# A two-layer attention kernel: a reordered opening, and VectorE adds the row of maxima to five groups of sixteen in 27 inner blocks of layer 0

## The reference, cut to what matters

```
# layer 0
theta = theta_w @ x + theta_b      # 64 x 4096, queries
phi   = phi_w @ x + phi_b          # 64 x 4096, keys
g     = g_w @ x + g_b              # 64 x 4096, values
y     = softmax(theta^T phi) @ g^T
x     = W_w @ y^T + W_b + x
# layer 1
q, k, v = Wq @ x + bq, Wk @ x + bk, Wv @ x + bv
x     = x + (softmax(q^T k * 128**-0.5) @ v^T)^T
```

## Time and profile before

| | us |
|---|---|
| median of 3 runs | 3208.1 (3196.96 to 3208.27) |
| the profiled execution, its time | 3209.59 |
| the profiled execution, its span | 3207.8 |
| busy PE / POOL / DVE / ACT in the span | 3171.6 / 2916.0 / 2104.9 / 1828.9 |

### The profile page before, as it was taken

How to read it: one execution, slowest core, us unless ns; L and a number is a source line. 1 busy time by engine, 2 the same in 40 slices (tenths; PEclk the granted TensorE clock), 3 DMA queues, 4 the chain that set the end, 5 groups by cost and what they waited for, 6 DMA issues and landing times. The chain is left out here.

```text
span 3207.8 us, 42372 instructions
## 1 busy us (share of the span) xinstructions
PE 3171.6 (99%) x15748; PEld 2088.9 (65%) x15748; DVE 2104.9 (66%) x2588; ACT 1828.9 (57%) x2378; POOL 2916.0 (91%) x1546
## 2 busy tenths in 40 slices
PE   8999999999999999999999999999999999999997
PEld 4555555547777765555777776555577777777775
DVE  4555555557777765555777776555577777777773
ACT  3545455555666655554666665555466666666665
POOL 3999999988999999998899998999899999999997
PEclk9999999999999999999999999999999999999999
DMA  1000000005756640000665654000066675657575
GB/s 52 21 27 27 24 27 27 27 27 109 144 115 140 136 99 21 27 27 27 128 141 112 144 119 102 27 27 24 26 142 129 132 145 114 134 118 145 114 141 119
DMA packets 91934, 271.68 MB, mean 85 GB/s; under 512 B 10192, under 2 KB 10192, under 8 KB 91728
## 3 DMA queue, kind: packets, MB, share of 16 engines
q0 software_dynamic: 55296, 201.35, 32.5%
q1 hardware_dynamic: 36432, 67.62, 7.1%
HBM read 50.83 MB, written 16.78 MB: 21 GB/s over the span
## 5 line engine op out<-in xcount | busy, mean ns | idle before, releaser
L1134 POOL TENSOR_TENSOR p_lo<-probs,p_hi 128x1024 fp32r<-128x1024 f32 x448 | 1160.9, 2631 | 110.3 <-ACT probs L895 76.3
L390 POOL TENSOR_TENSOR sums<-sums,probs 128x1024 f32<-128x1024 f32 x448 | 1067.5, 2383 | 104.5 <-ACT probs L901 53.3
L991 DVE TENSOR_REDUCE piece_max<-rough 128x2 f32<-128x1024 f32 x504 | 616.8, 1224 | 463.1 <-PE rough L546 463.0
L901 ACT ACTIVATE probs<-scores 128x1024 f32<-128x1024 f32 x512 | 519.7, 1025 | 638.3 <-PE scores L579 619.2
L1015 DVE TENSOR_TENSOR probs<-scores,shift_rows 128x1024 f32<-128x1024 f32 x512 | 626.6, 1224 | 369.7 <-PE scores L592 362.0
L894 ACT ACTIVATE p_hi<-probs 128x1024 fp32r<-128x1024 f32 x448 | 475.0, 1060 | 569.2 <-DVE probs L1015 568.9
L985 DVE TENSOR_REDUCE piece_max<-rough 128x1 f32<-128x512 f32 x1024 | 661.9, 683 | 125.8 <-PE rough L540 125.8
L895 ACT ACTIVATE probs<-probs 128x1024 f32<-128x1024 f32 x512 | 535.3, 1046 | 89.1 <-DVE probs L1015 89.1
L588 PE MATMUL scores<-qry_a,keys_a 128*128 128x512 f32 x1024 | 441.9, 432 | 0.0
L1168 POOL DMA_DIRECT2D sent_sums<-probs x384 | 409.2, 1066 | 0.0
L592 PE MATMUL scores<-qry_b,keys_a 128*128 128x512 f32 x1024 | 400.1, 391 | 0.0
(11 more groups left out here) (97 smaller groups left out, 4041.0 us busy)
## 6 DMA issues: line engine op xcount, KB each, us to landing
sent_sums<-probs POOLq DMA_DIRECT2D x384, 512.0 KB, 4.9
x_q<-x SPq DMA_DIRECT2D x32, 256.0 KB, 2.8
x_res<-x SPq DMA_DIRECT2D x32, 256.0 KB, 3.2
mid<-mid_new SPq DMA_DIRECT2D x32, 256.0 KB, 2.4
x_kv<-mid SPq DMA_DIRECT2D x32, 256.0 KB, 2.9
x_q<-mid SPq DMA_DIRECT2D x32, 256.0 KB, 2.8
x_res<-mid SPq DMA_DIRECT2D x32, 256.0 KB, 4.7
out<-result SPq DMA_DIRECT2D x32, 256.0 KB, 3.8
```

The costliest lines, as they stand in the source:

```text
L390: eng.tensor_tensor(sums[:], sums[:], probs[:, slot(st, s)], ALU.add).then_inc(s_plus, 1)
L901: nc.scalar.activation(probs[:, slot(st, s)], scores[:, s % 2], ACT.Exp, scale=SCALES[0]).then_inc(s_whole, 1)
L991: nc.vector.reduce_max(piece_max[:, t, TPG * c:TPG * (c + 1)], src, AX.X).then_inc(s_reduced, 1)
L1134: nc.gpsimd.tensor_tensor(dst, w, rd(hi), ALU.subtract).then_inc(done, 1)
```

## The change

A table `MOVED = (2, 6, 8, 12, 14)` names five groups. In the blocks of layer 0 whose next block is also of layer 0 and whose previous block is not of layer 1 (8 + 7 + 6 + 6 = 27 of the 32 blocks of layer 0) these groups get three products instead of four. DVE adds `shift_rows` on the way from PSUM to `probs` (`move_scores`), and ACT takes exp in place there (`probs_moved`). PE may write the PSUM buffer again when DVE has read it (`s_moved`). A pair inside a group (s = 5 and 11) now stands behind the third product instead of the second, in all blocks with such pairs.

The opening is written anew: the constants come in two DMAs (330 columns first, 640 later), the first queries are projected from x part 0, PE runs two products on constant tiles first and three more later that nothing reads (`busy`), pairs stand between the projections from the first chunks on, and the two small products move behind the next queries.

```diff
+MOVED = (2, 6, 8, 12, 14)
+        self.moved = MOVED if self.layer == 0 and self.by_pair and self.prev != 1 else ()
...
+                elif st.layer == 0 and s - 2 in st.moved:
+                    pe.wait_ge(s_moved, moved_until(st.g, s - 2))
...
-                    for n, (keys, qry) in enumerate(((hi[:, k], qa), (lo[:, k], qa), (hi[:, k], qb),
-                                                     (share[:], shift_rows[:, parity]))):
+                    products = [(hi[:, k], qa), (lo[:, k], qa), (hi[:, k], qb)]
+                    if s not in st.moved:
+                        products.append((share[:], shift_rows[:, parity]))
...
-                        if n == 2 and between is not None:
+                        if n == 3 and between is not None:
...
+            def probs_moved(st, s):
+                act.wait_ge(s_moved, moved_until(st.g, s))
+                place = probs[:, slot(st, s)]
+                nc.scalar.activation(place, place, ACT.Exp, scale=SCALES[0]).then_inc(s_whole, 1)
...
+            def move_scores(st, s):
+                dve.wait_ge(s_scores, st.g * GROUPS + s + 1)
+                probs_free_0(dve, st, s)
+                dve.wait_ge(s_row_sb, st.g + 1)
+                nc.vector.tensor_tensor(
+                    probs[:, slot(st, s)].rearrange("p (h c) -> p h c", c=QB),
+                    scores[:, s % 2].rearrange("p (h c) -> p h c", c=QB),
+                    rd(shift_rows[:, st.parity]).unsqueeze(1).to_broadcast([P, TPG, QB]), ALU.add).then_inc(s_moved, 1)
...
+            pe.wait_ge(s_set, 1)
+            pe.wait_ge(s_fill, 1)
+            busy(2)
+            pe.wait_ge(s_const, 16)
+            pe.wait_ge(s_x0[0], 16)
+            project(rough[:, 0:QB], wt_theta, first_image(0), p_q)
+            first_phi(0)
+            first_phi(1)
+            for c in range(0, BLOCKS, 2):
+                first_pair(2 * c)
+                first_g(c)
+                first_pair(2 * c + 1)
+                first_g(c + 1)
+                first_pair(2 * c + 2)
+                if c + 2 < BLOCKS:
+                    first_phi(c + 2)
+                    first_pair(2 * c + 3)
+                    first_phi(c + 3)
+                else:
+                    pe.wait_ge(h_phi, BLOCKS)
+                    busy(1)
+                    first_pair(2 * c + 3)
+                    busy(2)
+            pe.wait_ge(s_ones_r, 1)
             shift_row(0, 0)
             pe.wait_ge(s_reduced, PAIRS + 1)
             next_queries(1, 0, rough[:, 0:QB])
+            small_products()
```

More of the change, by code:

```diff
@@ L358, in probs_free_1, with moved_until @@
                 eng.wait_ge(s_plus, added(st.prev_nth, last))
+        def moved_until(g, s):
+            n = 0
+            for at in range(g + 1):
+                t, i = divmod(at, BLOCKS)
+                turn = (t >= 3 and i == 0) or (t >= 1 and i == BLOCKS - 1)
+                if layer_of(t) == 0 and not turn:
+                    n += len(MOVED) if at < g else MOVED.index(s) + 1
+            return n
         def shifted(nth, s):
@@ L427, in _ @@
         def _(sp):
-            sp.dma_start(const_sb[:], consts).then_inc(s_const, 16)
+            early = sum(w for _, w in CONST_PARTS[:FIRST_CONSTS])
+            sp.dma_start(const_sb[:, 0:early], consts[:, 0:early]).then_inc(s_const, 16)
             for k in range(X_PARTS):
                 sp.dma_start(probs[:, k], cols(x[0], k, GC)).then_inc(s_x0[k], 16)
-                if k == 0:
-                    sp.dma_start(x_q[:], cols(image(x, 0), 0)).then_inc(s_xq, 16)
+                if k == 1:
+                    sp.dma_start(const_sb[:, early:], consts[:, early:]).then_inc(s_late_const, 16)
             def load_q(g, layer, b, i):
@@ L579, in score_group @@
                             last = mm(scores[:, s % 2, h * QB:(h + 1) * QB], keys[half(h)], qry[half(h)],
-                                      start=n == 0, stop=n == 3)
+                                      start=n == 0, stop=n == len(products) - 1)
                     last.then_inc(s_scores, 1)
@@ L667, in out_projection, with small_products, busy, first_phi @@
                 mm(acc_out[:, parity], wt_out, o_sb[:], start=True, stop=True).then_inc(s_wy, 1)
[L670 to L688, removed]
+            def small_products():
+                pe.wait_ge(s_late_const, 16)
+                mm(rough[:, QB:QB + 2], wk, ones[:, 0:2], start=True, stop=True)
+                mm(rough[:, QB + 2:QB + 4], wt_out, g_bias, start=True, stop=True).then_inc(s_small, 1)
+            def busy(n):
+                for _ in range(n):
+                    mm(scores[:, 0, 0:QB], ones[:], total[:], start=True, stop=True)
+            def first_phi(c):
                 if c >= 2:
                     pe.wait_ge(h_phi, c - 1)
-                    pe.wait_ge(h_g, c - 1)
                 if c % 2 == 0:
@@ L907, in _ @@
             act.wait_ge(s_const, 16)
-            act.wait_ge(s_vec, 2)
             take_q_hi(0, 0, 0, rough[:, 0:QB])
-            for c in range(BLOCKS):
-                if c >= 2:
-                    act.wait_ge(l_phi, c)
-                take_phi(c, 0, c, scores[:, c % 2, 0:QB], (whole, x_kv)[c % 2])
-                take_g(c, g_first, c, scores[:, c % 2, QB:GC])
+            for c in range(0, BLOCKS, 2):
+                for n in (c, c + 1):
+                    if n >= 2:
+                        act.wait_ge(l_phi, n)
+                    take_phi(n, 0, n, scores[:, n % 2, 0:QB], (whole, x_kv)[n % 2])
+                for n in (c, c + 1):
+                    take_g(n, g_first, n, scores[:, n % 2, QB:GC])
             shift_to_row(0, 0)
             take_q_hi(1, 0, 1, rough[:, 0:QB])
+            act.wait_ge(s_vec, 2)
             def block_program(st):
@@ L945, in block_program @@
                         take_output(g, parity)
-                    if st.layer == 0:
+                    if s in st.moved:
+                        probs_moved(st, s)
+                    elif st.layer == 0:
                         probs_direct(st, s)
@@ L1078, in _ @@
                 reduce_pair(m, pair, pair_banks[m % 2])
+                if m == 0:
+                    dve.wait_ge(s_late_const, 16)
+                    nc.vector.tensor_scalar(neg_ident[:], idt, -1.0, None, ALU.mult).then_inc(s_neg, 1)
+            dve.wait_ge(s_neg, 1)
             shift(0, 0)
+            dve.wait_ge(s_small, 1)
+            nc.vector.tensor_copy(K_S, rough[:, QB:QB + 1]).then_inc(s_vec, 1)
+            nc.vector.tensor_tensor(OUT_B, rough[:, QB + 2:QB + 3], vec[:, 7:8], ALU.add).then_inc(s_vec, 1)
+            dve.wait_ge(s_vec, 2)
             split_q(1, 0, 1, rough[:, 0:QB])
@@ L1107, in block_program @@
                         m += 1
+                    if s in st.moved:
+                        move_scores(st, s)
                     if st.layer == 1:
```

39 lines of the change are left out of this document (25 added, 14 removed).

## The result

The changed kernel took 3285.47 us as a median of 4 runs (3277.27 to 3285.75), against 3208.18 (3196.96 to 3209.16) before: a ratio of 1.0243, 95% interval 1.0222 to 1.0263. It is 77 us slower. The executions of the kernel before fall into two groups, and in the 48 that were timed beside the experiments 32 lie at 3208.0 to 3210.7 and 16 at 3196.2 to 3198.1; the profiled one is of the longer kind. The direction and the two gaps were forecast; the size, 3257 with a range of 3212 to 3282, was not.

A forecast was written before the change was run, and what follows sets the result against it. PE was taken to bound the kernel, busy 99% of the span. From 3208.1 us, new gaps less saved products add 60.5 over 27 blocks and the opening gains 12: 3256.6 us, range 3212 to 3282.

The forecast's parts named there:

- the two gaps: New PE waits in a layer 0 block: 1.6 us at the next block's first pair, 1.5 us at group 9.
- The bound and its reading: Layer 0 inner blocks: PE busy 41.0 of 41.0 us, so any chain through DVE and ACT that lengthens opens a gap.
- The saving: Five products fewer on PE at 0.23 us each: 1.16 us a block, 31 us over 27 blocks.
- Group 14 and the block's end: Add behind `diag` delays both exps, the row and the queries; next block's first pair waits 1.6 us.
- the knock-on of 12: Groups 12 and 13: 0.25 us gap at group 15, plus 0.1 to 0.2 on the block-end chain; together 0.4 us.
- Groups 6 and 7: Add of 6 behind the reciprocals, exp of 7 behind four diagonals: group 9 waits, gap 1.5 us a block.
- The sum of a later block: New gaps of 3.5 us minus 1.16 saved: each block 2.3 us longer, between 1.2 and 2.7.
- The opening: the step that failed: Products on constants lift PE to the upper clock level: first score at 38 instead of 49.98, a 12 us gain.
- The forecast's low case: Opening stays at the lower clock level: a gain of only 4 us, total 3265.
- POOL: POOL's own block of about 40.2 us stays hidden, waiting more than 2 us a block after the change.
- The rival of a single gap: Only one of the two large block gaps opens: 3218 or 3205 us, counted as no change; chance 0.10.
- the rival of the middle: Only the gap at groups 6 and 7 opens: 0.3 us a block, 3205 us; within a shared chance of 0.10.

The follow-up runs named there:

- three groups: Kernel before, with its old opening, with only groups 2, 8 and 12 moved: 3198.5 us, ratio 0.9972.
- g first: Changed kernel, but in stage 0 ACT copies the g projection ahead of exp of group 14: 3268.4 us, ratio 1.0199.
- the add first: Changed kernel, but DVE adds group 6 ahead of the reciprocals and ACT writes the diagonals one group later: 3272.2 us, ratio 1.0212.
- without constants: Changed kernel with groups 2, 8, 12 moved (stage 0: 2 and 8) and no products on constants in the opening: 3200.9 us, ratio 0.9984.
- the three groups with the new opening: Changed kernel with groups 2, 8 and 12 moved in later blocks, only 2 and 8 in stage 0: 3194.7 us, ratio 0.9957.

## Why the prediction was wrong

*The bound and its reading.* Right. PE without a gap and chains with under 1 us of slack: each of these turned into a gap once it got 1.2 us longer.

*The saving.* Right: 0.23 us a product. The block with no group moved was 0.1 shorter besides (40.86 instead of 40.95); its one change is the place of the pair, which I had set to nothing.

*Group 14 and the block's end, later stages.* Right in place and size. Without group 14 the later block loses 1.6 us (43.50 to 41.90), the product of 0.23 given back included; 1.6 plus the knock-on of 12, less that product, had been worked out.

*Groups 6 and 7.* Right: 1.4 us a block (43.50 to 42.11) for 1.5 - 0.23.

*The sum of a later block.* 2.3 forecast, 2.55 measured (43.50 - 40.95). By the three runs with a group left out, group 14 cost 1.8 and group 6 1.6 before their product is taken off, 0.1 to 0.2 more each than in the sum, and group 12 0.2 instead of 0.4: three groups save 0.48 (40.95 - 40.47) and not 0.69.

*Stage 0: the step that failed.* I walked one block, of stage 1, and priced stage 0 with it. Stage 0 prepares phi and g instead of keys and values, and there ACT's queue holds a copy of g behind exp of 14, and PE's row product shares g's bank. The forecast had written "who waits" for the row, the queries and the pair, and not for what else ACT does at s = 14. In a block of stage 0 group 14 cost 2.3 us instead of 1.6 (44.77 - 42.68, and the product of 0.23; 2.1 of it is the idle time before the row), the copies of phi behind group 12 cost 0.7 instead of 0.4 (three moved groups save nothing there) and group 6 1.6 instead of 1.5: 4.6 - 1.16 = 3.5 us a block instead of 2.3. Two blocks with a clock fall of 1.6 come on top: 29.2 us instead of 16.8 for the stage. The run with g first shows that place by itself, and that behind it the queries' chain would still have cost 44.1.

*The opening: the step that failed.* 12 us of gain were forecast and 1.7 us lost. The work was right: where PE stays at the upper level the first score stands at 39.1 (forecast 38), the first pair at 9.6 to 10.6 (forecast 10.3). The level was wrong. I took it that a dense run ahead would bring the rest of the opening to the upper level; the runs show that it brings it for some microseconds, and that it is a draw how long it lasts: the level first fell at 12 us in the changed kernel, near 18 without group 14, near 23 with g first and near 30 with the add first. The rows that I had already spoke against it: the old opening ran at the lower level through 28 us without a gap of PE. The forecast's low case, 4 us of gain, was not low enough either: at the lower level PE waits 1.00 us for phi's copies in each of three rounds, a pair between projections takes 0.72 us (14.85 to 15.57) where the first of two pairs took 0.60 before (26.52 to 27.12), and the first score comes at 51.97 (51.55 without constants), 2 us later than in the old order. Nor is 49.98 the whole truth on the old opening: a third of the executions of the kernel before are 12 us shorter. No trace shows one of them, so that their opening ran at the upper level is likely and not shown. The Trainium skill, in "TensorE: Matmul & The Clock Gate", Part 1, says that activity lifts the rate. The trace agrees for the first pair (0.49 at 10.62), and not for the 28 us of the old opening, where the measurement decides.

*POOL.* It kept out of the way, as forecast: its block of 40.2 us lies under 43.5.

*The rival of a single gap, 3205 to 3218.* It did not come, but its prices can be compared. With the block's end alone (no group 6) 3244 were measured, with the middle alone (no group 14) 3233. These kernels each keep one product more on PE than the rivals, 6 us, and the rival of the middle left out the gap of group 12. The rest of the distance is stage 0's terms and the opening.

## What to carry to other kernels

Before an operation is moved to a half free engine, list what stands behind its result in every queue that it passes, up to the instruction of the bound engine that waits, and walk it with durations from the trace; the engine's busy share says nothing on this. Do it for each kind of block, since another stage may have one more copy in the queue at the same place. Then choose the places: of the five moved groups, three shorten the kernel and two cost some 80 us between them (48 and 32 in the blocks).

Where TensorE starts at the lower level, a reordering of the opening should be judged over many runs and by its spread, and a gain that hangs on the upper level should not be counted before durations in several executions show it.

## What the runs showed of the hardware

PE's level after a dense start is not settled by the program: one and the same opening gave first scores from 39.15 to 51.97 us, and whole runs 3185.9 to 3199.3. Nor does PE's busy time settle it: with 14.00 of 14 us busy the granted clock read 1.00, with 12.65 it read 0.57, with 12.00 it read 0.50, but with 11.00 of 13 busy the add first stayed at the upper level, and with 28.00 of 28 the kernel before stayed at the lower.

In the kernel before the column of the granted clock read 1.00 through the whole opening, where a pair's first products took 0.79 us instead of 0.50; there the durations tell the level.

A single idle time of 2.1 us in an otherwise full stretch was followed by products at half rate (granted 0.72 and 0.78 in the windows 229 to 232 and 232 to 236) in one of the changed kernel's blocks. Such a fall followed in 14 of 35 blocks of five executions, and nothing in the others.

```profile
229.00:232.00 3.00, 2.96 (x9) 0.77 (x9) 0.75 (x1) 1.97 (x3) 2.86 (x2) 0.72 0.04 14
232.00:236.00 4.00, 4.00 (x24) 2.45 (x24) 1.23 (x1) 1.69 (x2) 2.97 (x2) 0.78 0.00 0
```

The add on DVE took 1216 ns and exp from SBUF 1054, against 1224 and 1046 in layer 1: neither was disturbed by POOL's adds beside them, which took 2380 as before (2383).

What decides the draw in the opening, and behind the gap of 2.1 us, is left open. The four executions of g first lie within 0.9 us of each other, the seven of the three groups with the new opening over 13.
